# First experts stage: 47 row blocks instead of 48, and stores of finished rows issued by ScalarE instead of GpSimd

## The reference

```python
logits = jnp.einsum('sbd,de->sbe', x, Wg) + bg + bias
vals, idx = jax.lax.top_k(logits, TOP_K)              # TOP_K = 2, 16 experts
w = jax.nn.softmax(vals - jnp.max(vals, axis=-1, keepdims=True), axis=-1)
cw = jnp.einsum('sbk,sbke->sbe', w, jax.nn.one_hot(idx, NUM_EXPERTS, dtype=x.dtype))
h = jax.nn.relu(jnp.einsum('sbd,edh->esbh', x, W1) + b1[:, None, None, :])   # h: 512 wide
y = jnp.einsum('esbh,ehd->esbd', h, W2) + b2[:, None, None, :]
out = jnp.einsum('esbd,sbe->sbd', y, cw)
```

## Time and profile before

| | us |
|---|---|
| median of 3 runs | 1388.95 (1388.15 to 1389.63) |
| the profiled execution | 1391.05 |
| its span, first to last instruction | 1389.3 |
| PE busy | 1157.5 (83%) |
| DVE busy | 702.9 (51%) |
| ACT busy | 588.9 (42%) |
| POOL busy | 351.9 (25%) |
| DMA moved | 182.24 MB, mean 131 GB/s |

### The profile page before, as it was taken

One profiled execution on the slowest core, in us unless ns is written; L12 is line 12 of the kernel. 1 busy time (PEld: TensorE's weight loads), 2 busy tenths in 40 slices (PEclk: granted clock), 3 DMA queues, 4 the chain that ended last, 5 costly groups with the idle time before them and its releaser, 6 DMA issues. The chain is left out here.

```text
span 1389.3 us, 26425 instructions
## 1 busy us (share of the span) xinstructions
PE 1157.5 (83%) x8532; PEld 1010.5 (73%) x8532; DVE 702.9 (51%) x1546; ACT 588.9 (42%) x1194; POOL 351.9 (25%) x497
## 2 busy tenths in 40 slices
PE   5999987644599999247789856999999999999997
PEld 4787865633588888124545545999999999999997
DVE  6655554443122221255677856545555555555556
ACT  2666754111122222125577822434444444444432
POOL 5546540144011111446343012520000000000152
PEclk9999998578699999558899975999999999999999
DMA  7765760044799997363556321112322322322132
GB/s 190 151 194 146 195 215 2 0 134 154 281 330 320 331 330 277 95 136 66 80 84 86 59 99 46 68 60 78 102 77 93 105 84 80 112 79 82 49 88 88
DMA packets 88919, 182.24 MB, mean 131 GB/s; under 512 B 11747, under 2 KB 58525, under 8 KB 82448
## 3 DMA queue, kind: packets, MB, share of 16 engines
q1 hardware_dynamic: 76528, 141.40, 36.7%
q0 software_dynamic: 12320, 39.94, 8.5%
HBM read 134.29 MB, written 47.72 MB: 131 GB/s over the span
## 5 line engine op out<-in xcount | busy, mean ns | idle before, releaser
L2071 PE MATMUL e_ps<-xT_e,wp_e 128*128 128x384 f32 (+1 forms) x1344 | 245.1, 331 | 4.0 <-DVE wp_e L1945 4.0
L2071 PEld LDWEIGHTS e_ps<-xT_e,wp_e 128*128 128x128 f32 x1344 | 221.7, 188 | 5.4 <-issue 4.1
L725 DVE TENSOR_REDUCE att_ps<-att_ps 128x2 f32<-128x512 f32 (+1 forms) x224 | 154.8, 696 | 122.7 <-PE att_ps L1057 66.7
L970 ACT ACTIVATE probs<-att_ps 128x384 f32<-128x384 f32 (+1 forms) x256 | 129.9, 544 | 47.4 <-PE att_ps L1089 31.2
L1903 ACT ACTIVATE act_a_e<-e_ps 128x256 f32<-128x256 f32 (+2 forms) x176 | 77.8, 442 | 160.4 <-PE e_ps L2071 154.2
L2001 DVE TENSOR_TENSOR hid_e<-act_a_e,e_ps 128x256 f32<-128x256 f32 (+2 forms) x176 | 87.0, 494 | 115.8 <-ACT act_a_e L1903 99.1
L2088 PE MATMUL e_ps<-wp_e,hidp_e 128*128 128x256 f32 (+1 forms) x1008 | 138.3, 281 | 2.9 <-DVE xres L1961 1.2
L1907 ACT ACTIVATE hidp_e<-hid_e 128x256 fp32r<-128x256 f32 (+2 forms) x176 | 83.8, 476 | 126.9 <-DVE hid_e L2001 120.4
L2003 DVE TENSOR_TENSOR hidp_e<-hid_e,hidp_e 128x256 fp32r<-128x256 f32 (+2 forms) x176 | 87.9, 499 | 95.4 <-ACT hidp_e L1907 91.5
L2088 PEld LDWEIGHTS e_ps<-wp_e,hidp_e 128*128 128x128 f32 (+1 forms) x1008 | 130.5, 183 | 4.9 <-issue 4.1
L1055 PE MATMUL att_ps<-ks,qs 96*128 96x256 bf16 (+1 forms) x512 | 107.7, 279 | 31.3 <-DMA qs<-parts 21.3
(11 more groups left out here) (209 smaller groups left out, 1918.6 us busy)
## 6 DMA issues: line engine op xcount, KB each, us to landing
w_e<-in_W SPq DMA_DIRECT2D x48, 1024.0 KB, 7.7
w_e<-in_W SPq DMA_DIRECT2D x57, 384.0 KB, 3.0
ks<-parts SPq DMA_DIRECT2D x96, 128.0 KB, 4.3
qs<-parts SPq DMA_DIRECT2D x96, 128.0 KB, 7.4
parts<-cut SPq DMA_DIRECT2D x24, 384.0 KB, 3.0
rows<-zeros POOLq DMA_DIRECT2D x8, 768.0 KB, 7.3
x_e<-rows SPq DMA_DIRECT2D x48, 128.0 KB, 6.8
done<-y_e POOLq DMA_DIRECT2D x48, 128.0 KB, 6.5
```

The source lines that it names most:

```text
L725: dve.tensor_reduce(tops_at(at[3])[:, qt, x0:x0 + heads], src, AX.X, ALU.max).then_inc(reduced, 1)
L970: act.activation(probs[:, g % 2, x0, 0:WIDE], ps[:, TB + x0 % RING, 0:WIDE], ACT.Exp, scale=DK ** -0.5).then_inc(exped, 1)
L2071: last = pe.matmul(ps[:, bank + u % 2, 0:n], weights(lot, c, pw)[:, (b * DC + d) * P:(b * DC + d + 1) * P], xT[:, px, d, t0:t0 + n], start ...
```

## The change

- `NB0` is (2T + 16 * 127) // 128 = 47, the most blocks that 4096 pairs can fill when each expert's last block is padded. The loops run 11 rounds of four blocks and three blocks by hand, where they ran 12 rounds.
- ACT issues the stores of `y`. Its order is hide(n+2), store(n), where hide is the bias and relu of a block; the wait for `y_ready` stands in ACT's queue. POOL has no work in the stage.
- DVE waits for the landing (`y_stored[j]`) itself. `y_free` is gone.
- `rows0`, `done0`, the zero fill of `rows0` and four small routing operations over the blocks shrink by 1/48.

```diff
-NB0 = 2 * T // P + E0
+NB0 = (2 * T + E0 * (P - 1)) // P
...
+        ROUNDS = (NB0 - 1) // RING
+        LEFT = NB0 - RING * ROUNDS
...
-        @block.gpsimd
-        def _(pool):
-            lead(pool, y_free, RING)
-
-            def store(i, j):
-
-                n = RING * i + j
-                pool.wait_ge(y_ready, ready(n, 2))
-                pool.dma_start(ye[bass.ds(n * P, P), :], y[:, j]).then_inc(y_stored[j], 16)
-
-            def landed(i, j):
-
-                pool.wait_ge(y_stored[j], 16 * (i + 1))
-                pool.sem_inc(y_free, 1)
...
+            def hide(i, j):
+
+                n = RING * i + j
+                e = act.value_load(m["block_expert"][0:1, bass.ds(n, 1)], min_val=0, max_val=E0 - 1)
+                act.wait_ge(hid_made, ready(n, MADE))
+
+                act.wait_ge(y_made, free(n) + Y_MADE - 2)
+                for f in range(FC0):
+                    last = act.activation(hid[:, j % 2, f, :], ps[:, HB + j % 2, f * P:(f + 1) * P], ACT.Relu,
+                                          bias=b1[:, bass.ds(e, 1), f])
+                last.then_inc(hid_ready, 1)
+
+            def store(i, j):
+
+                n = RING * i + j
+                act.wait_ge(y_ready, ready(n, 2))
+                act.dma_start(ye[bass.ds(n * P, P), :], y[:, j]).then_inc(y_stored[j], 16)
+
+            hide(0, 0)
+            hide(0, 1)
+            with act.Fori(0, ROUNDS) as i:
                 for j in range(RING):
+                    hide(*at(i, j + 2))
+                    store(i, j)
+            for j in range(LEFT):
+                if j + 2 < LEFT:
+                    hide(ROUNDS, j + 2)
+                store(ROUNDS, j)
+            for j in range(RING):
+                act.wait_ge(y_stored[j], 16 * (1 + ROUNDS + (j < LEFT)))
...
+            for stored in y_stored:
+                lead(dve, stored, 16)
...
-                dve.wait_ge(y_free, free(n))
+                dve.wait_ge(y_stored[j], 16 * (i + 1))
```

More of the change, by code:

```diff
@@ L1525, in experts0_block @@
         turned, xT_ready, hid_made, hid_ready = sem("turned"), sem("xT_ready"), sem("hid_made"), sem("hid_ready")
-        y_made, y_ready, y_free = sem("y_made"), sem("y_ready"), sem("y_free")
+        y_made, y_ready = sem("y_made"), sem("y_ready")
         block = ctx.enter_context(nc.Block())
         TURNED, MADE, Y_MADE = RING, 2, RING
+        ROUNDS = (NB0 - 1) // RING
+        LEFT = NB0 - RING * ROUNDS
         def at(i, j):
@@ L1544, in _, with load @@
             sp.dma_start(b2[:].rearrange("p e d -> p (e d)"), a["b2"].rearrange("e d -> (e d)").partition_broadcast(P)).then_inc(b_loaded, 16)
-            with sp.Fori(0, NB0 // RING) as i:
-                for j in range(RING):
-                    n = RING * i + j
[L1548 to L1554, removed]
-        @block.gpsimd
-        def _(pool):
-            lead(pool, y_free, RING)
-            def store(i, j):
-                n = RING * i + j
-                pool.wait_ge(y_ready, ready(n, 2))
-                pool.dma_start(ye[bass.ds(n * P, P), :], y[:, j]).then_inc(y_stored[j], 16)
-            def landed(i, j):
-                pool.wait_ge(y_stored[j], 16 * (i + 1))
-                pool.sem_inc(y_free, 1)
[L1571 to L1581, removed]
+            def load(i, j):
+                n = RING * i + j
+                e = sp.value_load(m["block_expert"][0:1, bass.ds(n, 1)], min_val=0, max_val=E0 - 1)
+                sp.wait_ge(turned, free(n))
+                sp.dma_start(x[:, j], xe[bass.ds(n * P, P), :]).then_inc(x_loaded[j], 16)
+                sp.wait_ge(y_made, free(n))
+                sp.dma_start(w[:, j], a["W_0"][bass.ds(e, 1)].rearrange("a p f -> p (a f)")).then_inc(w_loaded[j], 16)
+            with sp.Fori(0, ROUNDS) as i:
+                for j in range(RING):
+                    load(i, j)
+            for j in range(LEFT):
+                load(ROUNDS, j)
         @block.scalar
@@ L1586, in _ @@
             act.wait_ge(b_loaded, 32)
-            with act.Fori(0, NB0 // RING) as i:
-                for j in range(RING):
[L1589 to L1597, removed]
+            def hide(i, j):
[8 more added lines that the diff above has]
+            def store(i, j):
+                n = RING * i + j
+                act.wait_ge(y_ready, ready(n, 2))
[3 more added lines that the diff above has]
+            with act.Fori(0, ROUNDS) as i:
+                for j in range(RING):
+                    hide(*at(i, j + 2))
+                    store(i, j)
+            for j in range(LEFT):
+                if j + 2 < LEFT:
[3 more added lines that the diff above has]
+                act.wait_ge(y_stored[j], 16 * (1 + ROUNDS + (j < LEFT)))
         @block.vector
         def _(dve):
+            for stored in y_stored:
+                lead(dve, stored, 16)
             lead(dve, y_ready, 2)
@@ L1615, in take_sums, with round_of @@
                 dve.wait_ge(y_made, ready(n, Y_MADE))
-                dve.wait_ge(y_free, free(n))
+                dve.wait_ge(y_stored[j], 16 * (i + 1))
                 dve.tensor_tensor(y[:, j], ps[:, YB + j % 2, 0:D], b2[:, bass.ds(e, 1), :].rearrange("p a d -> p (a d)"),
                                   ALU.add).then_inc(y_ready, 1)
-            def round_of(i, more):
-                for j in range(RING):
-                    if j + 2 < RING or more:
+            def round_of(i, known):
+                for j in range(min(known, RING)):
+                    if j + 2 < known:
                         take_rows(*at(i, j + 2))
@@ L1628, in _ @@
             take_rows(0, 1)
-            with dve.Fori(0, NB0 // RING - 1) as i:
-                round_of(i, True)
-            round_of(NB0 // RING - 1, False)
+            with dve.Fori(0, ROUNDS) as i:
+                round_of(i, RING + 2)
+            round_of(ROUNDS, LEFT)
         @block.tensor
@@ L1665, in second, with round_of @@
                 last.then_inc(y_made, 1)
-            def round_of(i, more):
-                for j in range(RING):
-                    if j + 1 < RING or more:
+            def round_of(i, known):
+                for j in range(min(known, RING)):
+                    if j + 1 < known:
                         first(*at(i, j + 1))
-                    if j + 2 < RING or more:
+                    if j + 2 < known:
                         turn(*at(i, j + 2))
@@ L1678, in _ @@
             first(0, 0)
-            with pe.Fori(0, NB0 // RING - 1) as i:
-                round_of(i, True)
-            round_of(NB0 // RING - 1, False)
+            with pe.Fori(0, ROUNDS) as i:
+                round_of(i, RING + 2)
+            round_of(ROUNDS, LEFT)
 def experts1_block(nc, m, a, hall, xe, ye, out, sw, sw_loaded):
```

## The result

The changed kernel takes 1376.18 us (median of 4 runs, 1375.12 to 1377.96), the kernel before beside it 1389.29 (1388.15 to 1390.31). The ratio is 0.9907, with an interval of 0.989 to 0.9924, so 10.6 to 15.3 us are gained, 13.1 by the medians. The forecast was 3.6 us, 1385.35, with a range that ended at 1378.5. The direction was right, the size was off by a factor of more than three.

The account below looks back on a forecast made before the run. The experts 0 stage was taken as paced by its weight loads, with PE 5% behind. Terms -3.9 + 1.2 - 0.9 = -3.6 us took 1388.95 to 1385.35 us, range 1378.5 to 1388.3.

Parts of the forecast that it names:

- One block fewer: Experts 0 stage: one pipeline turn less, worth 3.94 us paced by loads or 3.73 by PE; taken as -3.9 us.
- The stall: PE waiting for weights in experts 0: 0.21 us a block over 47 intervals, 9.9 us in all.
- The tail: End of experts 0, last sum to next stage's first load: ACT's last store lands earlier than POOL's; -0.9 us.
- The store as DMA work: Experts 0: ACT's stores take 0.3 to 0.95 engine-us more than GpSimd's, slowing the loads; +1.2 us.
- The later moment of the store: Experts 0: ACT's store goes out some 2.1 us later, behind hide; no cost, as DVE has 3 us left.
- ACT and DVE: Experts 0: ACT's store issue fits in its waiting time, and DVE's direct wait for the landing costs nothing.
- The rivals: Other outcomes for experts 0: faster loads, chance 0.17; block's gain eaten by split stores, 0.17; slower through ACT's queue, 0.05.
- the loads get faster: Experts 0: moving stores off GpSimd's queue and later frees the loads, PE sets the pace; 9.7 us more, chance 0.17.
- its half case: Half of the faster loads' gain in experts 0, giving 1379.5 us, the result expected if that rival (chance 0.17) holds.

Follow-up runs that it names:

- e1: Against the kernel before: 47 blocks instead of 48, with the stores still on GpSimd and y_free kept; ratio 0.9966 (0.994 to 0.9991).

## Why the prediction was wrong

*One block fewer: right.* Forecast -3.9. It is -3.73 at PE's pace, and e1 as a whole measured -4.7 (-8.3 to -1.3). The stall had been read too small, 9.9 us for 11.9, since the short last interval was counted as a full one.

*The tail: the first step that failed.* Forecast -0.9 with bounds of 0.5 and 1.4, measured -4.9, the largest part of the gain. The issue and the landing of a store were sized well: ACT's last store was issued 0.1 us after the end of its sum and landed 1.7 us later, for a forecast of 2.05. What was missed stood in the same rows. GpSimd's last store had landed at 560.9 and SP began at 565.23, 4.3 us that nothing accounted for. I compared them with the barrier before and took its 5.57 us for the bare cost of a barrier. But in that stage GpSimd issues 32 DMAs of its own, which at 0.08 us would be 2.6 of those 5.57 us; that is an estimate, since no run changed their number. A reference point that carries the same cost hides it.

*The store as DMA work: the second step that failed, with the wrong sign.* Forecast +1.2 with bounds of 0 and 2.7, measured -2.5 in the first pair of profiles and -3.9 between the means of the groups. The miss is as large as that of the tail. The price of a store in engine time was right, 6.05 for a forecast of 6.2, but that a busy share of 0.96 makes engine time the limit was not. With two more buffers the same engines kept PE at its full pace. The stage was limited by the lead of the loads, as I had read at first from 7.7 us against 7.46, and then I priced the store by bandwidth all the same. The later moment of the store, which I had worked out at 2.1 us, I priced at nothing in the forecast, and some 3 us of stall go with it. By the Trainium skill's overhead for small packets, page "DMA: Bandwidth & Descriptors", section "Why small descriptors are slow", I had estimated 7% more engine time for a store. The trace has 15% more, 6.05 us for 5.25, in three times the packets, and they went with less stall. (The rows had allowed 6.2 against 5.25 at most, which is 18% and not the 15% of the prediction; SP's 384 KB stores come from SP too and were left out there.)

*ACT and DVE: right.* PE never waited for ACT, DVE never for a landing. ACT's DMA issue takes 0.34 us as on SP, and it ran beside the activations.

*The rivals.* The measured time lies where "the loads get faster" had put it, 1374.5 to 1379.5 (its half case sums to 1379.3). That is in part luck. Of its 9.7 us at most 3.9 are there, from the moment of the store, which it had named, some 3, and from the queue no more than scatter. The largest single part of the gain is the tail, which no rival had.

*The sum after the fact.* -3.73 for the block, -3.9 for the stall, -4.9 for the tail are -12.5 us, against a measured 13.1 (10.6 to 15.3). With the tail as the other profiles have it, 7.0 less 2.7, the sum is -11.9.

## What to carry to other kernels

Where one engine ends a stage for all, account for the whole time between its last landing and the next stage before calling it a barrier; a DMA on GpSimd can cost more than its issue there, and 47 of ScalarE's did not (0.5 us from the last landing to the next stage, for 4.2). SyncE was never the last to finish in this stage, so these runs say nothing of it. A high DMA share doesn't say that bandwidth is the limit (PE's stall went at 0.97 and 0.98): give the loads a longer lead and see whether the stall goes. Only then is a price in engine time worth working out.

## What was not expected of the hardware

- Where GpSimd was the last to leave the stage, the next one began later by 0.08 us for each DMA that GpSimd had issued: 0.7, 2.4 and 4.3 us from the last landing to SP's load for 3, 23 and 47 DMAs. The size of the DMA didn't matter (8 KB or 128 KB, of 128 rows both), nor that all but three had landed 60 us earlier. What it does in that time, the profile doesn't show.
- ACT's sequencer issued a store while ACT's activations were running. In the change's timeline ACT issues at 406.93 for 0.34 us, and three activations run from 406.37 for 0.88 us. So the store goes out before the hide that stands ahead of it has ended, and PE never waited for ACT in the stage.
- Issuing the same store 1.6 us later left PE's stall about 3 us shorter over 46 blocks (8.2 for 11.2 in the means), with the weights landing in 7.0 to 7.4 us in place of 7.8. The cause stays open.
